# Dummy products in a two-block token kernel: one for three in the layers, none at the feed-forward, five for eight at the attention, five while the tokens are reloaded

## The reference

```python
h = _L0_tok_ref(x, ...)                 # windows of 8x8 pixels -> 64 tokens, by attention
h = jnp.concatenate([h, txt], axis=1)   # + 128 text tokens
h = h + _L0_attn_ref(_layernorm(h), ...)  # linear in, 4 state-space layers, linear out
h = h + _L0_ffn_ref(_layernorm(h), ...)   # gated feed-forward, half of the tokens chosen
h = h + _L1_attn_ref(_layernorm(h), ...)  # causal attention, 8 heads
h = h + _L1_ffn_ref(_layernorm(h), ...)   # 64 experts, top 2
```

```python
y = einsum('bnh,n->bh', state, Cbar) + u @ DT
new_state = einsum('nm,bmh->bnh', A, state) + (u @ BT)[:, :, None]
...
y = gelu(y) + h; return _ln(y)
```

## Time and profile before

| | |
|---|---|
| time before, median of 3 runs | 584.19 us (580.19 to 697.4) |
| profiled execution: its own time | 583.9 us |
| its span, first to last instruction | 582.1 us |
| TensorE, mean granted clock | 0.813 of 2.4 GHz |
| TensorE busy (products) | 433.9 us, 75% of the span |
| VectorE, ScalarE, GpSimd busy | 272.1, 158.8, 93.7 us |
| chain that ended last: TensorE, VectorE, ScalarE, GpSimd | 62%, 19%, 5%, 5% |
| dummy products (89 of them, 178 records) | 89.5 us busy |

### The profile page before, as it was taken

The page is one execution under the profiler, slowest core; times in us unless marked ns, Lnnn a source line. Parts: engine busy times, 40 slices in busy tenths (PEclk is TensorE's granted clock), DMA queues, the critical chain, the costliest instruction groups (busy, mean ns, idle before and its releaser), DMA issues.

```text
span 582.1 us, 10312 instructions
## 1 busy us (share of the span) xinstructions
PE 433.9 (75%) x4226; PEld 282.8 (49%) x4226; DVE 272.1 (47%) x669; ACT 158.8 (27%) x333; POOL 93.7 (16%) x106
## 2 busy tenths in 40 slices
PE   9764979774488884784899999999985449988300
PEld 5643737452345442352546777777734233377200
DVE  1355475562333446435726666666533542056222
ACT  2233527252122121032024444444400000044100
POOL 3101010000301112103120000000001057200275
PEclk9567868796599997665599999999976568999755
DMA  8360000000800000000190000000010000033111
GB/s 330 150 239 2 3 2 6 1 18 7 207 1 1 2 0 1 0 0 28 29 423 11 5 3 5 5 5 5 5 30 2 0 16 28 30 99 99 44 40 34
DMA packets 19735, 27.83 MB, mean 48 GB/s; under 512 B 12680, under 2 KB 17416, under 8 KB 19048
## 3 DMA queue, kind: packets, MB, share of 16 engines
q1 hardware_dynamic: 16144, 23.86, 12.0%
q0 software_dynamic: 1536, 1.58, 1.1%
q10 hardware_dynamic: 2016, 1.84, 0.9%
HBM read 21.50 MB, written 6.03 MB: 47 GB/s over the span
## 4 chain that ended last, share of the span: by engine, by line
PE 62%; DVE 19%; ACT 5%; POOL 5%; issue 4%; DMA 3%; DVEq 1%; POOLq 0%; SPq 0%; ACTq 0%
PE bank L1163 52%; PE bank L1166 9%; POOL windows L504 4%; DVE q_sum L784 2%; DVE windows L1134 1%; POOL rstd L451 1%; ACT xT L614 1%; DMA hL<-tokens_in 1%; DVEq L1131 1%; ACT xT L726 1%; DVE sc_sb L807 1%; DVE sc_sb L811 1%; DVE head_buf L791 1%; DVE mx_sb L810 1%; DVE sc_sb L818 1%
## 5 line engine op out<-in xcount | busy, mean ns | idle before, releaser
L1163 PE MATMUL bank<-windows 65*64 65x64 f32 (+3 forms) x976 | 94.0, 263 | 2.4 <-DVE windows L1134 1.9
L1163 PE MATMUL bank<-zero 128*64 128x512 f32 x178 | 89.5, 657 | 3.5 <-DVE hL L1119 2.0
L1163 PEld LDWEIGHTS bank<-windows 65*64 65x64 f32 (+3 forms) x976 | 65.2, 150 | 4.6 <-ACT windows L722 3.1
L1163 PEld LDWEIGHTS bank<-zero 128*64 128x64 f32 x178 | 25.5, 151 | 60.7 <-issue 57.5
L451 POOL TENSOR_TENSOR rstd<-ln_v,mhalf 128x6 f32<-128x6 f32 x16 | 21.1, 1326 | 186.0 <-DVE ln_v L877 186.0
L1032 DVE TENSOR_REDUCE xT<-bank 96x2 f32<-96x384 f32 (+1 forms) x48 | 26.5, 552 | 43.7 <-PE bank L1163 43.7
L1166 PE MATMUL bank<-w_tok,xT 128*128 128x128 f32 (+2 forms) x104 | 19.2, 323 | 32.9 <-DVE xT L882 20.8
L689 ACT ACTIVATE head_buf<-head_buf 96x384 f32<-96x384 f32 x48 | 25.1, 523 | 64.9 <-DVE head_buf L1035 64.9
L1166 PEld LDWEIGHTS bank<-w_tok,xT 128*128 128x128 f32 (+2 forms) x104 | 13.0, 153 | 46.0 <-issue 18.5
L1163 PE MATMUL bank<-xT 64*64 64x64 f32 (+2 forms) x192 | 31.6, 310 | 1.5 <-issue 0.7
L1166 PE MATMUL bank<-w_tok,windows 128*128 128x128 f32 (+1 forms) x184 | 29.0, 301 | 3.6 <-ACT xT L531 2.8
(11 more groups left out here) (212 smaller groups left out, 643.5 us busy)
## 6 DMA issues: line engine op xcount, KB each, us to landing
big<-in_x SPq DMA_DIRECT2D x4, 2048.0 KB, 11.8
big<-in_w_experts SPq DMA_DIRECT2D x1, 6144.0 KB, 17.7
x_slots<-zero SPq DMA_DIRECT2D x1, 1792.0 KB, 10.7
windows<-x_slots SPq DMA_DIRECT2D x14, 128.0 KB, 2.1
y_slots<-windows ACTq DMA_DIRECT2D x14, 128.0 KB, 1.7
w_ssm<-in_w_ssm SPq DMA_DIRECT2D x1, 448.0 KB, 8.6
hL<-tokens_in SPq DMA_DIRECT2D x2, 192.0 KB, 2.4
tokens_in<-hL SPq DMA_DIRECT2D x2, 192.0 KB, 1.8
```

The costliest lines, as they stand in the source:

```text
L1163: return nc.tensor.matmul(out, lhsT, rhs, start=start, stop=stop, **kw)
```

## The change

Three numbers and two calls of `keep_warm` on TensorE's program change. In each of the 8 half-layers one dummy product stands for three. Ahead of `ffn_in(0)` there are none for ten. Between the turns of tokens ahead of the attention there are five for eight. Five new ones stand behind the wait for `hn_ready`, ahead of `linear_in(0)`, at the place where the tokens are on their way through DRAM. The other calls are as before. In all there are 65 dummy products for 89. Nothing on another engine or queue changes, and nothing in what is computed.

```diff
-WARM_SSM, WARM_ATT, WARM_QKV = 3, 8, 4
+WARM_IN, WARM_SSM, WARM_ATT, WARM_QKV = 5, 1, 5, 4
...
             pe.wait_ge(s["hn_ready"], PAIRS)
+            keep_warm(WARM_IN)
             linear_in(0)
             turn_inputs(0, 0)
...
             linear_out(1)
-            keep_warm(WARM_NORM)
             ffn_in(0)
```

## The result

The changed kernel takes 564.76 us (median of 4 runs, 559.82 to 569.07) beside 583.3 for the kernel before (median, four runs). The ratio is 0.9665, with a 95% interval from 0.9602 to 0.9727. Run again later (e12) it was 565.19 (median), ratio 0.9648 [0.9592, 0.9704]. The forecast was 564. A ratio leaves out the runs that are over 1.5% longer than the shortest of their kernel (697.4 and 569.07 here); the medians are over all runs.

A forecast was written before the change was run, and what follows sets the result against it. The prediction took TensorE's dummies, where they end last, to bound the kernel around the layers, feed-forward and attention. 583.9 - 7.2 - 9.1 - 2.7 - 1.2 = 563.7, forecast as 564 us, range 558 to 571.

The forecast's parts named there:

- The layers: Half-layers, three dummies to one: 7.2 us less, as VectorE's norm is next; bounds 5.4 to 14.5.
- the first turn: From (0, layer 0) to (1, layer 0): transposes need only add_bin(1), so the full 1.81 us is saved.
- the releaser is the one named: Next half-layer's transposes should name VectorE's L882 as releaser, with about 0.9 idle.
- The feed-forward: Ahead of the feed-forward, ten dummies to none: 9.1 us less at the low clock, priced by half 1.
- The attention: Ahead of the attention, eight dummies to five: six quick records fewer, 2.7 us less.
- a cold start: Rival at the attention: five dummies too few or the clock falls, 2.7 given back, 566 us; chance 0.07.
- The reload: Five new dummies ahead of linear_in(0): cost 0, quicker first transposes and first projection, 1.2 us less.
- My bounds of 0 to 3.6: Reload's gain: 0 if the clock has fallen by 151.13, 3.6 us if it lasts until 160.2.
- The reading of the rows at 224 to 226: Behind the last half-layer's dummies the clock fell 2.4 us after their end; taken to favour the reload's smaller sum.
- The sign that I had named: Granted clock under 1.0 between first rise and last half-layer's end would make the forecast wrong upward.
- Falls now and then in the layers: Rival: one to four clock falls in the layers, 1.5 to 2 us each, 566 to 572, middle 569; chance 0.15.
- A loss of the clock for all the layers: Rival: every half-layer at the low clock with one dummy, 31 us more, 595; chance 0.04.

The follow-up runs named there:

- e12: The changed kernel once more, unaltered, as comparison for later runs: median 565.19 us, ratio 0.9648 to the kernel before.
- e1: The kernel before with one dummy for three in each half-layer, nothing else: median 576.34 us beside 584.95, ratio 0.989.
- e6: The changed kernel with two dummies for one in each half-layer: median 565.65 us, ratio 0.9653 to the kernel before.
- e8: The changed kernel with VectorE's norm of the other half moved ahead of this half's add_skip: median 556.93 us, ratio 0.9529.
- e2: The kernel before without the ten dummies ahead of the feed-forward: ratio 0.9894 to the kernel before.
- e3: The kernel before with five dummies for eight ahead of the attention: ratio 0.9943, median over all twelve runs 586.43 us.
- e10: The changed kernel with VectorE's norm ahead of add_skip and eight dummies for five in the reload: median 552.25 us, ratio 0.9444.
- e7: The changed kernel without the five dummies of the reload: median 566.11 us, ratio 0.9695 to the kernel before.
- e5: The changed kernel with no dummy in the layers: median 572.59 us, ratio 0.9801 to the kernel before.
- e11: The changed kernel with VectorE's norm ahead of add_skip and no dummy in the layers: median 556.35 us, ratio 0.9489.
- e9: The changed kernel with VectorE's norm ahead of add_skip and no dummies in the reload: median 556.98 us.
- e4: The kernel before with five dummies added during the reload, nothing else: ratio 1.0012 to the kernel before.

## Why the prediction was right, and where it was not

**The layers, 7.2 forecast, 7.05 measured.** Right step by step: 1.81 was forecast for the first turn and 1.72 measured (from the dummies' start to the transposes 1.00 after, 2.72 before); the releaser is the one named, with 0.77 idle where about 0.9 was forecast; e1 alone has the same 7.05, e6 shows the floor that VectorE sets, e8 removes it. Why the gain was not 14.5 is thus shown.

**The feed-forward, 9.1 forecast, 9.34 measured (9.3 in e2).** Right. Half 1's rows were the price of half 0 at the low level; only the start of the transposes, 0.2 earlier than I had set, is off.

**The attention, 2.7 forecast, 1.29 here and 2.4 in e3.** The mechanism is right. The size is nearly right where the clock doesn't fall. I had put 0.07 on a cold start; it came in two traces of ten with five dummies and costs some 1.7 (the four dummies behind the first products took 5.34 in place of 3.65), of the 2.7 that the prediction had for it. That the fall comes with five and not with eight isn't shown: four traces with eight are too few for it.

**The reload, 1.2 forecast, 0.71 longer measured.** This is the step that failed. Its first half came as written: from the first transposes to the first chunk product 4.17 (154.03 to 158.20) in place of 5.22, 1.05 gained. The failing sentence is "I take it that the level lasts for the first transposes and the first projection": it added a gain at the front and kept the rest of the stretch as it was before, with the clock's rise 9 us after the transposes. But in this trace the fall in the middle puts off the next rise to about 13, so `earlier_chunks` runs at 1.2 GHz (1.94 in place of 1.09) with what stands ahead of it, and more is lost than gained. My bounds of 0 to 3.6 had no loss in them. Of the seven traces with five dummies six lost 0.3 to 0.7 against those with none, and e8, with the shorter fall, gained 0.8 to 1.0. The reading of the rows at 224 to 226, a clock that falls soon after dummies end, was the right one, but I drew only the half of it: where the clock falls inside the half-layer, its next rise can come later than it would have without the dummies. The sign that I had named, a granted clock under 1.0 between the first rise and the last half-layer's end, did come, at 156.8. e10 shows the other side: with eight dummies and no gap the stretch is 9.19, 3.3 less than without any dummy, near the 3.6 that I had set as the most. The Trainium skill's page "TensorE: Matmul & The Clock Gate", section "Loop structure matters more than you think", says that products close behind each other stay warm. The trace of e10 agrees. With five dummies the wait ahead of the transposes was down to 1.77, and the whole 3.6 that I had worked out beside that rule did not come.

**The sum.** 20.2 were forecast. The stages from the reload to the attention have 17.1 less in the two traces, and 19.5 is the timed difference by the ratio (16 to 23). The forecast of 564 came out by steps of which the largest two, 16.3 together, were right to 0.25 each; the two small ones were 3.3 too hopeful together, and that lies within the scatter of the whole time. By the stages the sum would have been 583.9 less 17.1, 566.8; that the median came within 0.8 of 564 is in part luck.

**The rivals.** Falls now and then in the layers behind the first half-layer did not come with one dummy in seven traces (after, e1, e7 to e10, e12), but came three times with none in VectorE's old order (e5), and not with none in the new one (e11). A loss of the clock for all the layers never came: even e5 regained it each time. The Trainium skill's page "TensorE: Matmul & The Clock Gate", section "A second HAM failure mode: psum-queue depth-cycling", says that short idle pieces between groups of products can make the clock swing. The trace of e5 agrees, with 1.77 idle ahead of the transposes; the layers of the changed kernel, with 0.77, don't show it.

## What to carry to other kernels

Price a dummy by what ends last once it is gone: here VectorE's program order, which one moved line then freed for 5.0 us more. Let dummies that are to keep a clock up end where the real work begins: five that ended 2 us early were worth nothing in the whole time, eight that ended on the spot 2.6 us by the stages. Both are counts at one place; nothing between five and eight was run. A dummy inside another engine's wait cost nothing here, and without it the clock fell (e5), so take them away only down to that wait. Compare by stages, since the whole time of this kernel moves by some 10 us from run to run: between the traces up to 9 us of it lie ahead of the change, and up to 5.4 between the attention and the expert loop.

## What the runs showed of the hardware that I had not expected

The stage of the windows, the same code in all the kernels, ended between 138.76 (e2) and 147.81 (e9) in the traces, 9 us apart. The work by stretch, of e2 and then of e9 (its us, busy by engine with the number of records, then the clock), tells whose time it is:

```profile
0.00:138.70 138.70, 102.53 (x1742) 72.94 (x1742) 69.94 (x132) 51.86 (x112) 13.46 (x32) 0.83 0.21 79
```
```profile
0.00:147.80 147.80, 111.27 (x1742) 79.73 (x1742) 69.95 (x132) 52.57 (x112) 13.46 (x32) 0.76 0.20 74
```

TensorE has the same 1742 records in both and is busy for 8.7 us more, at a mean granted clock of 0.76 in place of 0.83; VectorE and GpSimd have the same busy time. So the same products meet the low level more often in one execution than in another. The whole time goes the same way. Of the 29 runs of the kernel before that were timed beside e1 to e4 (580.02 to 591.06), the four shortest have a mean granted clock of 0.819 to 0.822 and the four longest one of 0.799 to 0.805.

In the first half-layer a clock that was brought up and then fell cost more than one that was never up: 12.8 to 13.0 us against 12.3 to 12.5 for the same stretch, in six traces of seven with five dummies. The seventh (e8), with the shorter fall, took 11.5.
